# Two feed-forward layers whose weights are split in place, from scratch copies that the attention's last steps make

## The chip, the cores and the metric

The kernel runs as one program on one core of one Trainium2 chip. The metric is the device time of one execution in microseconds (us), taken as the median of several runs. The trace comes from one profiled execution. Engines are named as in the profile: PE (TensorE) multiplies, PEld is its weight load, DVE is VectorE, ACT is ScalarE, POOL is GpSimd, and SP is the queue that issues most DMAs.

## The reference

Two transformer layers over x, 4096 tokens of 256 features, all in float32. Each sublayer takes a layer norm of x and adds its output to x.

```python
x = x + _L0_attn_ref(_layernorm(x), Wq, bq, Wk, bk, Wv, bv, Wo, bo)   # 16 heads of 16, full softmax over 4096
x = x + _L0_ffn_ref(_layernorm(x), gate_w, w1, b1, w2, b2, sw1, sb1, sw2, sb2)
x = x + _L1_attn_ref(_layernorm(x), ...)                              # linear attention with a gate
x = x + _L1_ffn_ref(_layernorm(x), router_w, router_b, w1, b1, w2, b2, sw1, sb1, sw2, sb2)
```

The first feed-forward has a shared expert `relu(x @ sw1 + sb1) @ sw2 + sb2` with 1024 hidden columns, and two experts of the same size, of which each token takes the one that its gate scores higher. The second has a shared part of 2 x 512 hidden columns with silu, and 64 experts of 64 hidden columns, of which each token takes eight with their softmax weights. Together the weights of the two feed-forward layers are 6 MB and 10 MB.

## The kernel before

The program is a row of phases, each with its own semaphores: `setup_phase`, `qkv0_phase`, `attention_phase`, `ffn0_phase`, `qkv1_phase`, `kv1_phase`, `out1_phase` and `moe_phase`. A phase ends with a barrier over all engines, POOL clears the phase's semaphores, and there is a second barrier (`PhaseSemaphores.__exit__`, lines 93 and 94). A phase that calls `sem.start()` then gives all its semaphores a first value of one: POOL adds it to one after the other (line 86), and a barrier follows (line 87), before which no engine does anything of the phase. Six phases do so, with 32, 24, 37, 21, 39 and 50 semaphores (qkv0, attention, ffn0, qkv1, out1 and moe).

Every product of the feed-forward layers is made of three matmuls with operands cut in a high and a low part (`product3`, lines 56 to 58): ACT copies the float32 value to a high part in fp32r, and DVE subtracts that from the value and writes the low part. Weights need the same cut once. `WeightCut` does that through a small ring of staging places: SP loads item n to place n mod ring (line 938) when DVE has done with item n - ring, ACT writes the high part (942), DVE the low part (946). Each item is 128 partitions x 1024 values, 512 KB, with a few smaller ones. `weights.ready` makes an engine wait for the low part of the last item.

**Attention.** 64 steps, eight pairs of heads by eight blocks of 512 keys. PE makes the scores for the maximum (line 724) and for the exponential (737, 745) and the product with the values (757), DVE takes the maxima (837), ACT the exponentials (814). Per step SP issues, in this order: the loads of the keys of the block three steps ahead (`load_k`, lines 659 and 664), in two steps of sixteen also the next pair's queries (`load_q`), and then `load_shift` (682 and 688), which brings the negated maxima of the next step into the rows of its keys when POOL has cut them; PE waits for that before the next step's exponential scores. POOL stores NUM and DEN at each step's end. SP's stream of the last sixteen steps is written out separately from the loop before it.

**ffn0_phase.** Eight blocks of 512 tokens. Before the first block, the "front" of block 0 runs: reciprocal of den, quotient, its cut (`o_hi`, `o_lo`), the output projection, the sum x1, the layer norm (mean, centre, square, variance, std, reciprocals, scale, hi, lo) and the gate. SP loads num, den, x, then nine bias and gate columns, and then the twelve weight items over three staging places. ACT and DVE wait for all nine columns first, do the weights' cuts with parts of the front between them, and PE begins block 0 after `weights.ready`. In a block, 24 chunks of 128 hidden columns go through `hidden` (6 matmuls), ACT twice, DVE, and `output` (6 matmuls) two chunks later; for the 16 routed chunks DVE first makes `chosen`. Between the chunks of a block stands the front of the next one, at fixed chunks. The blocks run in a loop of two per turn, and the last two are written out (`overlapped`).

**moe_phase.** Eight blocks again, of 40 chunks (8 shared, 32 pairs of experts), and a router. SP loads seven biases, and 23 weight items over four staging places, one of which is the buffer of x; when all cuts are done (`weights.ready(sp)`) it loads x of block 0 (line 1751). Then come the layer norm of block 0, the router's products (`head`) and the chunks. Per chunk ACT makes the silu (1883), DVE multiplies it by the token's weight for routed chunks (1981), ACT cuts the high part (1889), DVE the low part (1984), and PE makes `output` of the chunk two before.

qkv1_phase and out1_phase load four and three biases at their start, and wait for them only when they come to use them.

## Time and profile before

| | us |
|---|---|
| median of three runs | 4902.59 (4899.29 to 4906.36) |
| the profiled execution | 4904.38 |
| its span, first to last instruction | 4902.7 |
| PE busy | 4503.7 (92% of the span) |
| DVE busy | 3647.4 (74%) |
| ACT busy | 3162.0 (64%) |
| POOL busy | 538.8 (11%) |
| first DMA of ffn0, of qkv1, of moe | 2803.48, 3463.42, 3797.22 |

PE is busy 92% of the span, and the stretches where it isn't lie at the ends and starts of the phases. The mean granted TensorE clock is 0.955 of full speed. The DMAs move 165 MB in all, a mean of 34 GB/s. A busy share is a mean over phases with different limits, so the places where PE stands still are to be read one by one.

### The profile page before, as it was taken

The page shows a single profiled execution, that of the slowest core. Times are in us where ns is not written, and L with a number is a line of the kernel's source. Part 1 is how long each engine was busy: PE and PEld are TensorE (multiplying, and loading weights), DVE is VectorE, ACT ScalarE, POOL GpSimd, SP SyncE. Part 2 cuts the span into 40 slices and gives each one's busy share as a digit, 9 for nine tenths or more (in the row PEclk, how much of TensorE's full clock was granted, in tenths as well). Part 3 has the DMA queues.
Part 4 walks back from the last instruction along what each step waited for, and adds up shares of the span by engine and source line. Part 5 has one row for each costly group of instructions (what it writes and reads, how often), then busy time and mean ns, then how long its engine had stood idle before and what let it go on. Part 6 is the DMA issues. An engine that isn't in the chain of part 4 may idle for free. (4 is left out here: it accounts for less than half of the span.)

```text
span 4902.7 us, 107872 instructions
## 1 busy us (share of the span) xinstructions
PE 4503.7 (92%) x36227; PEld 2730.8 (56%) x36227; DVE 3647.4 (74%) x3699; ACT 3162.0 (64%) x5605; POOL 538.8 (11%) x1382
## 2 busy tenths in 40 slices
PE   6589999999999999999999789999874499999999
PEld 4344444444444444444444367777553378778777
DVE  4599999999998999999999765655446444444454
ACT  2158888888887888888888644444553344444444
POOL 3501111111111111111111100000000000000000
PEclk8789999999999999999999889999987699999999
DMA  4611110201202002120020120000101400000000
GB/s 162 197 29 21 26 25 18 34 18 22 34 17 34 18 18 34 21 33 21 18 33 18 39 69 26 28 23 14 36 13 60 96 13 13 13 13 13 13 5 14
DMA packets 216402, 165.36 MB, mean 34 GB/s; under 512 B 127728, under 2 KB 167328, under 8 KB 215104
## 3 DMA queue, kind: packets, MB, share of 16 engines
q1 hardware_dynamic: 199584, 151.15, 13.1%
q0 software_dynamic: 16384, 8.42, 0.7%
q8 instruction: 273, 4.47, 0.4%
q14 instruction: 161, 1.32, 0.1%
HBM read 103.63 MB, written 55.05 MB: 32 GB/s over the span
## 5 line engine op out<-in xcount | busy, mean ns | idle before, releaser
L837 DVE TENSOR_REDUCE PM<-A 128x2 f32<-128x1024 f32 x2092 | 2456.7, 1220 | 91.0 <-PE A L724 58.2
L814 ACT ACTIVATE PR<-SB 128x512 f32<-128x512 f32 x4100 | 2120.8, 603 | 360.6 <-PE SB L737 347.2
L757 PE MATMUL PV<-PR,VH 128*32 128x256 f32 x16384 | 1292.5, 386 | 2.4 <-issue 2.4
L724 PE MATMUL A<-QST,KA 48*128 48x512 f32 x4184 | 1193.2, 475 | 66.8 <-DMA QF<-QFD 41.7
L757 PEld LDWEIGHTS PV<-PR,VH 128*32 128x32 f32 x16384 | 432.9, 110 | 555.3 <-issue 367.8
L724 PEld LDWEIGHTS A<-QST,KA 48*128 48x128 f32 x4184 | 426.7, 187 | 524.0 <-issue 454.6
L737 PE MATMUL SB<-KST,QST 50*128 50x512 f32 x3075 | 687.6, 411 | 0.2
L737 PEld LDWEIGHTS SB<-KST,QST 50*128 50x128 f32 x3075 | 386.6, 186 | 207.8 <-ACT PR L814 204.8
L1984 DVE TENSOR_TENSOR m_h_lo<-m_h_full,m_h_hi 128x512 fp32r<-128x512 f32 x320 | 221.5, 692 | 285.1 <-ACT m_h_hi L1889 284.8
L745 PE MATMUL SB<-KF,QF 99*32 99x512 bf16 x4100 | 415.7, 384 | 5.5 <-issue 4.3
L1889 ACT CAST m_h_hi<-m_h_full 128x512 fp32r<-128x512 f32 x320 | 198.5, 620 | 245.5 <-DVE m_h_full L1981 243.4
L1981 DVE TENSOR_TENSOR m_h_full<-m_h_full,m_c 128x512 f32<-128x512 f32 x256 | 175.2, 684 | 235.4 <-ACT m_h_full L1883 205.0
L1883 ACT ACTIVATE m_h_full<-m_h,m_b 128x512 f32<-128x512 f32 x256 | 175.6, 686 | 195.3 <-PE m_h L58 194.6
L1195 DVE SCALAR_TENSOR_TENSOR chosen<-gate_out,h_ps 128x512 f32<-128x512 f32 x128 | 87.1, 680 | 181.3 <-PE h_ps L58 181.3
L896 POOL DMA_DIRECT2D NUM<-OS x256 | 126.6, 494 | 864.2 <-ACT OS L825 721.0
L1134 ACT ACTIVATE h_full<-chosen,b 128x512 f32<-128x512 f32 x128 | 92.4, 722 | 198.1 <-DVE chosen L1195 197.4
L56 PE MATMUL m_h<-ln_hi,moe_w_hi 128*128 128x512 f32 x512 | 208.7, 408 | 0.0
L57 PE MATMUL m_h<-ln_lo,moe_w_hi 128*128 128x512 f32 x512 | 202.8, 396 | 0.0
L56 PE MATMUL m_y<-m_h_hi,moe_w_hi 128*128 128x512 f32 x512 | 201.9, 394 | 0.0
L58 PE MATMUL m_h<-ln_hi,moe_w_lo 128*128 128x512 f32 x512 | 201.8, 394 | 0.0
L58 PE MATMUL m_y<-m_h_hi,moe_w_lo 128*128 128x512 f32 x512 | 201.5, 394 | 0.0
L57 PE MATMUL m_y<-m_h_lo,moe_w_hi 128*128 128x512 f32 x512 | 200.3, 391 | 0.0
(297 smaller groups left out, 5548.2 us busy)
## 6 DMA issues: line engine op xcount, KB each, us to landing
QST<-QS SPq DMA_DIRECT2D x54, 256.0 KB, 8.9
KA<-KAD SPq DMA_DIRECT2D x402, 32.0 KB, 1.8
KST<-KS SPq DMA_DIRECT2D x402, 32.0 KB, 1.9
QS<-parts SPq DMA_DIRECT2D x16, 512.0 KB, 5.7
KS<-parts SPq DMA_DIRECT2D x16, 512.0 KB, 4.7
KAD<-dealt SPq DMA_DIRECT2D x16, 512.0 KB, 3.5
m_x<-X3T SPq DMA_DIRECT2D x16, 512.0 KB, 3.7
KF<-KFD SPq DMA_DIRECT2D x402, 16.0 KB, 1.8
```

Of the source, the lines that this page charges most:

```text
L56: nc.tensor.matmul(out, w[0], x[0], start=first, stop=False)
L57: nc.tensor.matmul(out, w[0], x[1], start=False, stop=False)
L58: return nc.tensor.matmul(out, w[1], x[0], start=False, stop=last)
L724: return nc.tensor.matmul(A[:, u % 2 * 2 + e, :], keys, QST[rows, slot, j * TB:(j + 1) * TB], start=True, stop=True)
L737: nc.tensor.matmul(SB[:, s_bank(v), :], QST[rows, slot, c * P:(c + 1) * P], KST[rows, nb % K_SLOTS, :], start=True, stop=True).then_inc(s_ ...
L745: mm = nc.tensor.matmul(SB[r * 2 * HD:(r + 1) * 2 * HD, s_bank(v), :], QF[0:FINE_ROWS, slot, at:at + 2 * HD], KF[0:FINE_ROWS, nb % K_SLOTS ...
L757: mm = nc.tensor.matmul(PV[at:at + 2 * HD, 0:HB], VH[:, slot, e, c, :], PR[:, (2 * c + e) % P_SLOTS, b * HB:(b + 1) * HB], start=(c == 0), ...
L814: nc.scalar.activation(PR[:, v % P_SLOTS, :], SB[:, s_bank(v), :], ACT.Exp, scale=SCALE).then_inc(s_free, 1)
L837: nc.vector.tensor_reduce(PM[:, par, :, i, j:j + 1], A[:, u % 2 * 2:u % 2 * 2 + 2, :], AX.X, ALU.max).then_inc(a_free, 1)
L1883: nc.scalar.activation(h_full[:, c % RING, :], h_ps[:, c % 2, :], ACT.Silu, bias=bias).then_inc(full_ready, 1)
L1889: nc.scalar.copy(h[0][:, c % RING, :], h_full[:, c % RING, :]).then_inc(hi_ready, 1)
L1984: nc.vector.tensor_tensor(h[1][:, c % RING, :], h_full[:, c % RING, :], h[0][:, c % RING, :].bitcast(F32), ALU.subtract).then_inc(lo_ready, 1)
```

## The change

- `PhaseSemaphores.start` deals the first values out to five engines in turn.
- `weight_copies`: nineteen DMAs copy all feed-forward weights from the inputs to scratch tensors in device memory (F1, F2, RW, S1, S2, W1, W2). Eighteen of them make 16 MB, most of 1 MB each, and RW has 64 KB. W1 is stored as 256 rows of 4096 values, so its copy writes runs of 64 values (256 bytes).
- `constant_loads`: 21 DMAs load all later biases and gate columns to a lasting buffer `constants`. The loads of them in ffn0, qkv1, out1 and moe are gone, with their waits; only the two loads of `L1_ffn_b2` stay in moe.
- SP issues these 40 DMAs in the last sixteen steps of the attention, two or three after each step's `load_shift`, and waits for all of them at the end of its stream.
- `WeightCut` has no staging: an item is loaded from the scratch copy to the place of its low part, ACT writes the high part, and DVE subtracts in place. Each item has a semaphore of its own, and SP issues all loads without waiting.
- ffn0: items 0 to 3 (the shared expert) are cut between the parts of block 0's front, items 4 to 11 within block 0 at the chunks in `CUTS`, and PE waits per item (`ready(pe, n)`). The columns' differences and sums are made after `o_lo`. The first two blocks are written out.
- moe: x is loaded first. Items 0 to 3 are cut within block 0's layer norm, items 4 to 22 within block 0 (`CUTS`). The shared experts' weights now come ahead of the routed ones in the list. Tail 0 and head 1 are written out.
- Numbers of semaphores per phase as above: 32, 25, 45, 20, 38 and 69, of which each engine gives a fifth its first value.

```diff
+def overlapped_from_first(eng, body):
+    for slot in range(2):
+        body(0, slot, slot, 2)
+    with eng.Fori(1, NB // 2 - 1) as half:
...
     def start(self):
+        nc = self.nc
+        engines = (nc.gpsimd, nc.sync, nc.scalar, nc.vector, nc.tensor)
         for n, s in enumerate(self.held):
             if n not in self.from_zero:
-                self.nc.gpsimd.sem_inc(s, FIRST)
-        self.nc.all_engine_barrier()
+                engines[n % len(engines)].sem_inc(s, FIRST)
+        nc.all_engine_barrier()
...
+def weight_copies(d):
+    copies = [(d["F1"][0], d["L0_ffn_sw1"]), (d["F2"][0], d["L0_ffn_sw2"]), (d["RW"], d["L1_ffn_router_w"])]
+    for e in range(2):
+        copies += [(d["F1"][e + 1], d["L0_ffn_w1"][e]), (d["F2"][e + 1], d["L0_ffn_w2"][e])]
+        copies += [(d["S1"][e], d["L1_ffn_sw1"][e]), (d["S2"][e], d["L1_ffn_sw2"][e])]
+    per_expert = d["W1"].rearrange("n (e h) -> e n h", h=D // 4)
+    for g in range(0, 64, 16):
+        copies.append((per_expert[g:g + 16], d["L1_ffn_w1"][g:g + 16]))
+    for g in range(4):
+        rows = slice(g * 1024, (g + 1) * 1024)
+        copies.append((d["W2"][rows], d["L1_ffn_w2"].rearrange("e h n -> (e h) n")[rows]))
+    return copies
+
+def constant_loads(d, K):
+    loads = [(K["bo"], column(d["L0_attn_bo"])), (K["f0_b1"][:, 0:8], column(d["L0_ffn_sb1"])),
...
@@ attention_phase, SP, the last 16 of 64 steps @@
                         step(pair * NB + nb, pair, hp, nb, (pair + 1) % HPAIRS)
+                        for dst, src in early[hp * NB + nb::2 * NB]:
+                            sp.dma_start(dst, src, allow_slow_non_contiguous=True).then_inc(ahead_moved, 16)
+                sp.wait_ge(ahead_moved, count(16 * len(early)))
...
@@ class WeightCut @@
-    def load(self, sp):
-        ring = len(self.places)
-        for n, (src, _, _) in enumerate(self.items):
-            if n >= ring:
-                sp.wait_ge(self.lo_done, count(n - ring + 1))
-            sp.dma_start(self.staged(n), src).then_inc(self.loaded[n % ring], 16)
+    def load(self, sp, n):
+        src, _, low = self.items[n]
+        sp.dma_start(low.bitcast(F32), src).then_inc(self.loaded[n], 16)
 
     def hi(self, act, n):
-        act.wait_ge(self.loaded[n % len(self.places)], count(n // len(self.places) * 16 + 16))
-        self.nc.scalar.copy(self.items[n][1], self.staged(n)).then_inc(self.hi_done, 1)
+        act.wait_ge(self.loaded[n], count(16))
+        _, high, low = self.items[n]
+        self.nc.scalar.copy(high, low.bitcast(F32)).then_inc(self.hi_done, 1)
 
     def lo(self, dve, n):
         dve.wait_ge(self.hi_done, count(n + 1))
-        self.nc.vector.tensor_tensor(self.items[n][2], self.staged(n), self.items[n][1].bitcast(F32),
+        _, high, low = self.items[n]
+        self.nc.vector.tensor_tensor(low, low.bitcast(F32), high.bitcast(F32),
                                      ALU.subtract).then_inc(self.lo_done, 1)
 
-    def ready(self, eng):
-        eng.wait_ge(self.lo_done, count(len(self.items)))
+    def ready(self, eng, n):
+        eng.wait_ge(self.lo_done, count(n + 1))
...
@@ ffn0_blocks @@
+        CUTS = {2: 4, 3: 5, 4: 6, 6: 7, 9: 8, 10: 9, 11: 10, 14: 11}
...
                 load_sums(0)
                 load_x(0, 0)
-                col(bo[:, :], d["L0_attn_bo"])
...
-                weights.load(sp)
-                weights.ready(sp)
+                for n in range(PER):
+                    weights.load(sp, n)
+                for n in range(PER, len(items)):
+                    weights.load(sp, n)
                 sp.wait_ge(o_lo, count(1))
...
                 def hidden(i, slot, c):
+                    if first(i) and c % HC == 0:
+                        weights.ready(pe, c // HC * PER + 1)
...
                 def output(i, c):
                     e, k = divmod(c, HC)
+                    if first(i) and k % (HC // 2) == 0:
+                        weights.ready(pe, e * PER + 2 + k // (HC // 2))
...
+                for part in ("projection", "mean", "variance"):
+                    front(0, 0, part)
                 pe.wait_ge(diffed, count(4))
-                for part in ("projection", "mean", "variance", "gate"):
-                    front(0, 0, part)
-                weights.ready(pe)
-                overlapped(pe, blocks)
+                front(0, 0, "gate")
+                overlapped_from_first(pe, blocks)
...
-                for n in range(len(items)):
-                    weights.hi(act, n)
-                    front(0, 0, {1: "o_hi", 4: "square", 6: "std", 9: "hi"}.get(n))
-                overlapped(act, blocks)
+                for n, part in enumerate(("o_hi", "square", "std", "hi")):
+                    front(0, 0, part)
+                    weights.hi(act, n)
...
                 def blocks(half, i, slot, following):
                     for c in range(C):
+                        if first(i) and c in CUTS:
+                            weights.lo(dve, CUTS[c])
...
-                dve.wait_ge(consts, count(CONST_LOADS))
+                for part in ("den0", "den1", "den2", "den3", "quotient", "o_lo"):
+                    front(0, 0, 0, part)
...
@@ moe_phase and moe_blocks @@
+                cols = slice(g * G * EH, (g + 1) * G * EH)
+                items.append((d["W1"][k * P:(k + 1) * P, cols], *[v[:, k, cols] for v in w1]))
...
+        CUTS = {0: (4,), 1: (5,), 2: (6,), 3: (7,), 4: (8,), 5: (9,), 7: (10,), 10: (11,), 11: (12,), 12: (13,), 15: (14,),
+                18: (15,), 19: (16,), 20: (17,), 23: (18,), 26: (19,), 27: (20,), 28: (21,), 31: (22,)}
...
             head(0, False)
-            with eng.Fori(0, NB - 1) as i:
+            tail(0, True)
+            head(1, True)
+            with eng.Fori(1, NB - 1) as i:
...
-                weights.load(sp)
-                weights.ready(sp)
                 sp.dma_start(x[:, :, :], x3_dram[:, :, 0:TB]).then_inc(x_loaded, 16)
+                for n in range(2):
+                    weights.load(sp, n)
+                for p in range(2):
+                    sp.dma_start(b2_raw[p * 64:(p + 1) * 64, :], d["L1_ffn_b2"]).then_inc(bias_loaded, 16)
+                for n in range(2, EARLY):
+                    weights.load(sp, n)
+                for n in range(EARLY, len(items)):
+                    weights.load(sp, n)
...
-                for n in range(len(items)):
-                    weights.lo(dve, n)
-                weights.ready(dve)
                 ln.vector_centre(dve, 0)
+                weights.lo(dve, 0)
                 for part in range(2):
                     ln.vector_reciprocal(dve, 0, part)
                 ln.vector_scale(dve, 0)
+                weights.lo(dve, 1)
+                weights.lo(dve, 2)
                 ln.vector_lo(dve, 0)
+                weights.lo(dve, 3)
```

## Rows read from the trace of the kernel before

**Rows 1.** Windows: start and end us, length, busy us of each engine, clock, DMA share, GB/s.

```profile
2600.00:2700.00 100.00, 99.93 (x1124) 47.30 (x1126) 98.15 (x87) 86.35 (x169) 11.58 (x37) 1.00 0.08 15
2854.20:2932.20 78.00, 75.70 (x318) 59.78 (x319) 44.16 (x56) 34.73 (x52) 0.00 (x0) 0.99 0.11 34
3800.00:3850.00 50.00, 0.00 (x0) 0.00 (x0) 25.42 (x25) 21.87 (x24) 0.00 (x0) 0.50 0.99 214
3871.30:3999.30 128.00, 127.46 (x539) 102.52 (x540) 58.85 (x96) 58.49 (x87) 10.34 (x32) 0.97 0.02 5
```

**Rows 2.** Timeline of SP's queue, two attention steps: start us, us of issuing, DMA, how many.

```profile
2731.05 2.41 SPq L682 DMA_DIRECT2D KST<-NM  x4
2733.50 1.90 SPq L688 DMA_DIRECT2D KF<-NF  x3
...
2769.42 2.41 SPq L682 DMA_DIRECT2D KST<-NM  x4
```

**Rows 3.** Instructions of line 86 on POOL, whole span.

```profile
L86 POOLq EVENT_SEMAPHORE  x203: 17/17/17, 21.3 to 3796.9; - x102
```

**Rows 4.** Waits of SP: us in total, times, longest.

```profile
SPq L87 <- PEq L87: 17.2, 6, 4.1
```

**Rows 5.** Ends of the attention's streams, line 652: duration ns, start us.

```profile
L652 SPq DRAIN  x1: 369/369/369, 2773.8 to 2773.8; - x1
...
L652 POOLq DRAIN  x1: 10515/10515/10515, 2788.7 to 2788.7; - x1
```

**Rows 6.** Timeline, start of the first feed-forward: start us, us, instruction, idle before.

```profile
2803.93 0.46 SPq L1023 DMA_DIRECT2D den<-DEN  x1
...
2811.91 0.47 SPq L1019 DMA_DIRECT2D gate_cols<-in_L_ffn_gate_w  x1
...
2815.24 6.58 DVE L1155 RECIPROCAL den<-den 128x256 f32<-128x256 f32 x4
...
2823.12 1.04 ACT L1115 CAST ln_hi<-num 128x1024 fp32r<-128x1024 f32 x1 [4.53 <-DVE num L1158]
...
2825.27 1.22 DVE L1163 TENSOR_TENSOR ln_lo<-num,ln_hi 128x1024 fp32r<-128x1024 f32 x1
...
2841.25 0.69 ACT L172 ACTIVATE ln_sq<-front_ps,eps 128x512 f32<-128x512 f32 x1 [0.23 <-PE front_ps L137]
...
2849.78 1.23 DVE L163 TENSOR_TENSOR ln_lo<-ln_xc,ln_hi 128x1024 fp32r<-128x1024 f32 x1
...
2854.21 0.79 PE L56 MATMUL h_ps<-ln_hi,f_w_hi 128*128 128x512 f32 x1 [0.23 <-DVE f_w_lo L946]
```

**Rows 7.** Timeline, start of the mixture of experts.

```profile
3797.22 0.36 SPq L1743 DMA_DIRECT2D r_bias<-in_L_ffn_router_b  x1
...
3814.47 1.04 ACT L942 CAST moe_w_hi<-m_h_full 128x1024 fp32r<-128x1024 f32 x1 [0.53 <-DMA m_h_full<-in_L_ffn_w]
...
3815.55 1.23 DVE L946 TENSOR_TENSOR moe_w_lo<-m_h_full,moe_w_hi 128x1024 fp32r<-128x1024 f32 x1 [0.35 <-ACT moe_w_hi L942]
...
3849.52 0.37 SPq L1751 DMA_DIRECT2D m_x<-X3T  x1
3853.41 3.75 PE L130 MATMUL m_turn<-m_x,ones 128*128 128x512 f32 x4 [65.67 <-DMA m_x<-X3T]
...
3869.93 1.23 DVE L163 TENSOR_TENSOR ln_lo<-ln_xc,ln_hi 128x1024 fp32r<-128x1024 f32 x1 [1.11 <-ACT ln_hi L177]
3871.31 0.39 PE L56 MATMUL m_turn<-moe_rw_hi,ln_hi 128*128 128x64 f32 x1 [7.86 <-DVE ln_lo L163]
```

**Rows 8.** DMA issues: how many, KB each, median us to landing.

```profile
den<-DEN SPq DMA_DIRECT2D x8, 512.0 KB, 4.8
...
ln_sq<-in_L_ffn_w SPq DMA_DIRECT2D x4, 512.0 KB, 5.5
```

**Rows 9.** Groups by line: busy us, mean ns, idle before, releaser.

```profile
L1883 ACT ACTIVATE m_h_full<-m_h,m_b 128x512 f32<-128x512 f32 x256 | 175.6, 686 | 195.3 <-PE m_h L58 194.6
L1981 DVE TENSOR_TENSOR m_h_full<-m_h_full,m_c 128x512 f32<-128x512 f32 x256 | 175.2, 684 | 235.4 <-ACT m_h_full L1883 205.0 <-PE m_c L1802 30.4
```

More of the change, by code:

```diff
@@ L46, in feature_major @@
     return ap.rearrange("(k p) n -> p k n", p=P)
+def overlapped_from_first(eng, body):
+    for slot in range(2):
+        body(0, slot, slot, 2)
+    with eng.Fori(1, NB // 2 - 1) as half:
+        for slot in range(2):
+            body(half, half * 2 + slot, slot, 2)
+    for slot in range(2):
+        body(NB // 2 - 1, NB - 2 + slot, slot, 1 - slot)
 def column(ap):
@@ L1592, in _ @@
                 copy_o(0)
-                act.wait_ge(consts, count(48))
                 with act.Fori(0, NB // 2 - 1) as i:
@@ L1807, in output @@
                     w, k = (s2, c) if c < SC else (w2, c - SC)
+                    if first(i):
+                        weights.ready(pe, 1 + c // (SC // 2) * 3 + 2 if c < SC else 7 + k // 8 * 4 + 2 + k % 8 // 4)
                     pe.wait_ge(lo_ready, count(i * C + (c + 1)))
@@ L1834, in head @@
                 def head(i, finish):
+                    if first(i):
+                        weights.ready(pe, 0)
                     pe.wait_ge(ln.lo_ready, count(i + 1))
@@ L1879, in chunk @@
                 def chunk(i, c):
+                    if first(i):
+                        for n in CUTS.get(c, ()):
+                            weights.hi(act, n)
                     act.wait_ge(h_done, count(i * C + (c + 1)))
@@ L1977, in chunk @@
                 def chunk(i, c):
+                    if first(i):
+                        for n in CUTS.get(c, ()):
+                            weights.lo(dve, n)
                     if c >= SC:
@@ L2018, in _ @@
                                         ALU.subtract).then_inc(b_cut, 1)
-                for n in range(len(items)):
-                    weights.lo(dve, n)
-                weights.ready(dve)
                 ln.vector_centre(dve, 0)
+                weights.lo(dve, 0)
                 for part in range(2):
@@ L2044, in program @@
              "ones": sb("ones", [P, P], F32), "eps": sb("eps", [P, 1], F32)}
+        constants = sb("constants", [P, sum(CONSTANTS.values())], F32)
+        at = 0
+        for name, n in CONSTANTS.items():
+            K[name] = constants[:, at:at + n]
+            at += n
         with ExitStack() as weights:
```

161 lines of the change are left out of this document (81 added, 80 removed).

## The prediction

> **What bounds the kernel now.** I read the windows first, to see which stretches an engine fills. In the attention PE is busy 99.9 us of 100 and DVE 98 [rows 1]: nothing of this change touches either, so that phase can only be disturbed. In block 0 of each feed-forward phase PE is busy 75.7 of 78 us and 127.5 of 128 [rows 1]: PE bounds them. The 50 us in front of the second one are the opposite: PE does nothing, its clock is granted at 0.50, DVE and ACT are half busy, and the DMA engines are busy 99% of the time at 214 GB/s [rows 1]. That is the weight load with its small ring. So the gain must come from the time between a phase's barrier and PE's first block, and the timelines of the two starts [rows 6, 7] are where it is read. Between phases there is also the start barrier: SP waits there 17.2 us in six phases [rows 4], while POOL gives 203 semaphores their first value [rows 3].
>
> **Semaphores.** 17.2 us for 203 increments is 0.085 us each; some of that is the barrier, which stays, so I take 0.080. After the change the engines work side by side and the longest share counts: 7, 5, 9, 4, 8 and 14 increments, 47 in all. 156 fewer at 0.080 is 12.5 us: 2.2 in ffn0 (28 fewer), 2.9 in moe (36), 7.4 in the other four (92). All engines stand at this barrier, so all of it is on the path. The rate of the four other engines isn't shown. Below, it can be as fast as POOL or faster (1 to 2 us more at most); above, I allow twice POOL's time, 0.16 us each, and then 47 x 0.08 = 3.8 us are lost again. I take POOL's rate.
>
> **ffn0, up to block 0.** Now the first reciprocal of den starts at 2815.24, after the last gate column, which SP issued at 2811.91, though den was issued at 2803.93 [rows 6]. Afterwards nothing but den holds it. With the barrier 2.2 us earlier den is issued at 2801.7, lands 4.8 us later [rows 8], and the reciprocals start at 2806.5. From their start to PE's first product of block 0 are now 2854.21 - 2815.24 = 39.0 us [rows 6]. Of these go: 1.1 us between the end of `o_hi` (2824.16) and `o_lo` (2825.27), filled by two cuts of weights; about 1.8 us of the 9.1 between the end of std (2841.94) and that of the layer norm's low part (2851.01), since the two cuts between the reciprocals and one more are gone and one (1.2 us on DVE, beside 1.05 on ACT, so 0.2 net) stays; and 0.2 us of the last wait for the cut weights. That leaves 35.9, and block 0 starts at 2842.4, 11.8 us earlier. Items 0 to 3 are cut where DVE waits for PE or ACT anyway. The bound on the other side: twelve loads of weights are queued right behind den and x, and if they share the engines with den it lands like a weight load, 5.5 us, or up to 2 us later.
>
> **ffn0, in block 0.** Eight cuts, 1.23 us of DVE and 1.04 of ACT each (the size of those in [rows 7]), go into a block in which DVE is free for 33.8 of 78 us and ACT for 43.3 [rows 1]. On average they are hidden. But three stand at chunks 2, 3 and 4, where DVE has a reciprocal of 1.65 us too (6.58 for four [rows 6]) and a low part of 0.68: 3.6 us for a chunk, against 78 / 24 = 3.25 for the mean chunk with all its extra work, and less for these, which have none on PE. Chunk 10 has a cut, the two operations of x1, and two more of 0.7 each. `output` runs two chunks late, and that forgives one such delay but not three. Between 0 (the two chunks of slack take all) and 8 us (every cut waits about 1 us) I take 3.4. ffn0 gains 8.4.
>
> **moe, up to block 0.** SP's first DMA goes from 3797.22 to 3794.3, and it is x. Alone, x took from 3849.52 to PE's start at 3853.41, 3.9 us, and from there to the router's first product at 3871.31 it was 17.9 us [rows 7]. DVE has items 1 and 2 (half size, 0.68 us each) between scale and low part while ACT makes the high part: 0.3 us. The two `L1_ffn_b2` loads come behind x and two small items and are cut while PE makes the mean (3.75 us), so they cost nothing; if they land later than that they cost what they are late, up to 2 us. The router starts at 3794.3 + 3.9 + 17.9 + 0.3 = 3816.4 and no longer at 3871.3: 54.9 us earlier. What covers the load of 10 MB now is block 0 itself: at the 214 GB/s of before it takes 50 us, and its last item is cut at chunk 31 of 40, some 100 us into the block. The next block's x stands behind all weights in SP's queue, lands near 3850, and is asked for at chunk 12, about 3816 + 12 x 3.2 = 3855, with the router's products ahead of it some us more: 5 us to spare, no more. PE's clock is low when it starts on either kernel (0.50 before, and 0.97 is the mean of that block 0 [rows 1]), so it takes no part in the difference.
>
> **moe, in block 0.** Nineteen cuts into 128 us with 69 us of DVE and 69.5 of ACT free [rows 1]. Here ACT and DVE wait for each other in each routed chunk: cut 1.04, silu 0.69, DVE's product 0.68, high part near 0.65 make 3.1 us with its handovers near 3.6 [rows 7, 9], against 3.2 us a chunk (128 / 40). Runs of three cuts (chunks 10 to 12, 18 to 20, 26 to 28) get late by some 1.5 us, which the two chunks of lag forgive, except at 18 to 22, where the next layer norm's two reciprocals and scale are on DVE too: about 5 us late against 3 forgiven. With something for chunk 4, where ACT loads tables, I take 4, between 0 and 10 (half a us for each cut). moe gains 50.9.
>
> **The attention.** A step takes 38.4 us (2731.05 to 2769.42), SP's last shift of one is issued at 2735.4 and the next one not before 2769.4 [rows 2]; in between stand only key loads, which are wanted more than a step later. So the copies have 34 us a step, less some 3 for the key loads' bytes. The first steps copy two times 1 MB. The trace has no copy from device memory to device memory. The nearest rows are the weight loads, with 256-byte runs in moe, 214 GB/s together [rows 1]: 10 us for 2 MB. Even at a third of that the next shift goes undisturbed. POOL's stores may share the engines with key loads behind a copy, but POOL has nothing due for some 20 us. The last copy is issued when SP's stream ends now, 2773.8, and POOL drains from 2788.7 for 10.5 us [rows 5]; so SP's new wait is hidden by 25 us. I take nothing, with 3 us as the upper end (0.2 us a step).
>
> The Trainium skill ("DMA: Bandwidth & Descriptors", "Why a DMA increments its semaphore by 16 and not by 1") has a rule that could speak against this: a DMA is spread over the largest number up to 16 that divides the slowest dimension of both its sides, and a copy without such a dimension runs on one engine. By that rule these copies, with 256, 512 or 1024 rows or 16 experts ahead, get all sixteen, and the sum stays; were one flattened, the third rival below would be the result. No row here shows which, as all transfers of the trace have one side in SBUF.
>
> **Sum.** 7.4 + 8.4 + 50.9 = 66.7 us. The sum is made against the profiled execution, 4904.38, which is 1.8 above the median of the three runs; both move alike. 4902.6 - 66.7 = 4835.9. qkv1 and out1 gain nothing from their missing loads, since they wait for them behind their first work; the extra waits of PE and the larger clears (69 semaphores, not 50) are tenths. What this kernel's measurement can tell from no change is 0.2%, some 10 us.
>
> **Rivals.** First, the cuts in block 0 cost more than I give them. For it: the chunk of 3.6 us against 3.2, and runs of three. Against it: both engines are half idle in the block [rows 1]. If each of the 27 cuts holds PE for its 1.04 us of ACT, it is 28 us and not 7.4, so 4856; half of that, 4845. It shows as idle PE with DVE's low part as releaser. I give 4845 to 4858 a chance of 0.16.
>
> Second, queueing: num, den, x and b2 share the engines with the weight loads behind them, or the second block's x is late. Den and x would be 2 us late each, the second x by the 50 us load being, say, 65: 7 us. That gives 4840 to 4847, part of the range anyway. 0.10.
>
> Third, slower than before: a copy runs on too few DMA engines and the next `load_shift` stands behind it. 214 GB/s over sixteen engines is 13.4 GB/s each [rows 1]. On one engine 1 MB takes 78 us, all copies 1250 us, where sixteen steps last 614: the attention ends some 640 us later and the time is near 5475. It decides where two copies don't fit in 31 us, which is below 68 GB/s or five engines. Against it: key and weight loads are spread. 0.05.
>
> Fourth, the change doesn't do what it says, because PE's start in moe hangs on something else that I don't see, or the dearer side of the increments comes with the first rival: gain under 10 us 0.02, otherwise 4858 to 4880 0.04.
>
> **Chances and range.** My forecast, 4827 to 4845, has 0.63 (its lower end is with no stalls in both blocks: 4828). Slower by over 0.2% 0.05, within 0.2% 0.02, faster 0.93. With 0.63 + 0.10 + most of the first rival the range 4825 to 4855 holds 0.8 and more; its lower end takes in the stalls at zero and increments faster than POOL's, its upper end stalls of 8 and 10, increments at twice the price, and 2 us of queueing: 66.7 - 10.6 - 3.8 - 2 = 50.3, 4852.
>
> **What the profile would show.** SP's waits at the start barrier near 5 us in all. The first reciprocal of den near 2803 (2806.5 less the 3.5 us gained in the two phases ahead), and 35.9 us from it to the first product of block 0. In moe x as the first DMA, 22 us to the router, and block 0 at 128 us plus some 4 of idle PE. Attention steps of 38.4 us to the end. I am wrong if shifts land late (PE idle in the last sixteen steps), if PE's idle time in either block 0 is over 10 us, or if the router starts more than 24 us after SP's first DMA.

## The result, and the profile after

The changed kernel takes 4852.29 us, the median of four runs (4846.32 to 4852.49), against 4904.48 for the kernel before on the same chip: a ratio of 0.9894, with a 95% interval of 0.9882 to 0.9906. That is 52 us less; the prediction had 4836, or 67 us less. The profiled execution is the fastest of the four, 4846.32 us with a span of 4844.7, so it gained 58.0 us on the one profiled before.

To see where the 58 us come from, I cut both traces at the same events: the first and the last copy of an attention step's sums (ACT, `OS<-PV`), the first product of h in each feed-forward, the last store of X2T and moe's first DMA. The third column is the prediction's, with its semaphore term dealt out by the increments that each phase saves.

| stretch | before, us | after, us | gain forecast | gain measured |
|---|---|---|---|---|
| start to first copy of sums | 327.63 | 323.29 | 3.5 | 4.3 |
| first to last copy of sums | 2454.95 | 2460.03 | 0 | -5.1 |
| to ffn0's first product | 71.63 | 60.42 | 11.8 | 11.2 |
| to the last X2T store | 603.54 | 614.07 | -3.4 | -10.5 |
| to moe's first DMA | 339.47 | 332.02 | 6.8 | 7.5 |
| to moe's first product of h | 79.20 | 26.97 | 52.0 | 52.2 |
| to the end | 1026.28 | 1027.90 | -4.0 | -1.6 |

The waits of SP at the start barrier [rows 4], us in total, times, longest; then the start of ffn0 that answers to [rows 6] and that of moe that answers to [rows 7]:

```profile
SPq L100 <- PEq L100: 5.2, 6, 1.4
```

```profile
2802.53 0.39 SPq L1073 DMA_DIRECT2D num<-NUM  x1
2802.97 0.47 SPq L1074 DMA_DIRECT2D den<-DEN  x1
...
2807.65 6.59 DVE L1207 RECIPROCAL den<-den 128x256 f32<-128x256 f32 x4 [24.13 <-DMA den<-DEN]
...
2843.74 0.63 PE L67 MATMUL h_ps<-ln_hi,f_w_hi 128*128 128x512 f32 x1
...
3789.83 0.39 SPq L1789 DMA_DIRECT2D m_x<-X3T  x1
...
3793.78 3.78 PE L143 MATMUL m_turn<-m_x,ones 128*128 128x512 f32 x4 [11.59 <-DMA m_x<-X3T]
...
3811.68 0.39 PE L67 MATMUL m_turn<-moe_rw_hi,ln_hi 128*128 128x64 f32 x1 [7.86 <-DVE ln_lo L176]
```

The barrier wait fell from 17.2 to 5.2 us. The reciprocals of den wait for den alone, and from the first of them to block 0 it is 2843.74 - 2807.65 = 36.1 us. In moe the router starts 21.9 us after SP's first DMA. So both starts went as forecast, and the question is what happened in the two stretches with the large minus: the attention and ffn0's blocks.

PE's waits in moe's block 0 after the change, us in total, times, longest:

```profile
PE m_y L67 <- DVE m_h_lo L2045: 1.8, 3, 1.0
PE m_c L1852 <- DVE cw L2032: 1.0, 1, 1.0
```

These and two shorter ones make 3.4 us. The stretch from the router's first product of block 0 to that of block 1, before and after (columns as in [rows 1]):

```profile
3871.30:4002.40 131.10, 130.56 (x553) 105.01 (x554) 60.77 (x98) 59.56 (x88) 10.34 (x32) 0.97 0.02 5
3811.70:3946.50 134.80, 131.41 (x553) 104.30 (x554) 81.89 (x118) 76.12 (x108) 12.56 (x32) 0.97 0.11 37
```

It is 3.7 us longer, with PE idle for 3.4 us where it was 0.5. The six blocks between that and the last take 127.7 us each and not 128.0, and the last is 0.3 shorter too, so the last row of the table hides most of what block 0 lost: 3.7 lost, 2.1 gained. What made the later blocks shorter isn't isolated. The load of moe's weights moves 379 GB/s from 3799.8 to 3819.8, and the 10 MB are through some 34 us after moe's first DMA, where the prediction took 50 for them from the 214 GB/s of before. The DMAs of moe's start make 7985 packets now; they made 28642, of which 22880 were under 512 bytes. Which part of the speed comes from the copies' longer rows and which from the missing ring, no run separates.

The issues of the copies, size each and median us to landing, and SP's queue in one of the steps that carry them:

```profile
W<-in_L_ffn_w SPq DMA_DIRECT2D x4, 1024.0 KB, 6.1
S<-in_L_ffn_sw SPq DMA_DIRECT2D x4, 512.0 KB, 3.9
```

```profile
2736.09 0.60 SPq L772 DMA_DIRECT2D W<-in_L_ffn_w  x1
2737.05 3.32 SPq L772 DMA_DIRECT2D constants<-in_L_ffn_b  x1
...
2770.10 2.42 SPq L736 DMA_DIRECT2D KST<-NM  x4
```

A copy of 1 MB lands in 6.1 us, 172 GB/s for one DMA, so by estimate it runs on many engines: the 214 GB/s of [rows 1] are 13.4 for each of sixteen. The next shift is due 34 us later. The fifteen steps from the sixteenth-last copy of sums to the last take 578.2 us, as before (578.1). What the prediction cited from the Trainium skill ("DMA: Bandwidth & Descriptors", on the spreading over the slowest dimension) agrees with this landing, which doesn't tell many engines from all sixteen.

ffn0's blocks are read from SP's stores of X2T, start us and us of issuing:

```profile
3003.45 0.40 SPq L1089 DMA_DIRECT2D X2T<-f_x  x1
3081.07 0.40 SPq L1089 DMA_DIRECT2D X2T<-f_x  x1
3158.40 0.40 SPq L1089 DMA_DIRECT2D X2T<-f_x  x1
```

The distances are 77.62 and 77.33 us. In the trace of before the same stores stand 76.61 and 76.33 apart, and so on in turn for all: seven blocks cost 7.2 us more, although neither the code of those blocks nor the granted clock (1.00) differs. In the attention the loss isn't at the copies at all. It lies ahead of them, mostly in steps 15, 31 and 47, the ones at which the engines' loop of sixteen steps jumps back or ends. The turn at step 15 in windows (engines' busy us, PE's clock, DMA share, GB/s), and PE's two waits in it, at 906 and at 927 us:

```profile
905.00:910.00 5.00, 4.07 (x27) 2.03 (x27) 2.45 (x2) 2.10 (x4) 2.91 (x6) 0.50 0.33 76
...
925.00:930.00 5.00, 2.77 (x22) 1.84 (x22) 1.16 (x2) 0.85 (x2) 0.00 (x0) 0.83 0.27 49
930.00:935.00 5.00, 5.00 (x34) 2.12 (x35) 3.11 (x4) 2.88 (x6) 0.00 (x0) 0.50 0.00 0
935.00:940.00 5.00, 5.00 (x47) 2.26 (x39) 3.20 (x3) 2.88 (x7) 0.00 (x0) 0.64 0.00 0
940.00:945.00 5.00, 5.00 (x60) 2.54 (x58) 4.68 (x6) 4.26 (x9) 1.29 (x7) 1.00 0.06 5
```

```profile
PE A L781 <- issue: 3.4, 1, 3.4
PE PV L814 <- issue: 2.8, 1, 2.8
```

PE stands still twice with nothing to wait for but its own next instruction: for 3.4 us at the jump, and for 2.8 us some 20 us behind it, in the middle of a step. Each time the clock is then granted at 0.50, the lower of its two levels (1.2 GHz), over the next window. With both, this step takes 51.9 us and not 38.5. The kernel before has the same turns, at 43.1, 48.7 and 47.6 us; its stands at the jumps are 2.8, 2.8 and 3.1 us, and the second stand is missing in its first turn, the shortest.

### The profile page after: what moved, and what is told of

It is laid out like the page before. It is cut to its first block and busy times, and to the rows that moved or that the text cites. A ratio compares the mean times of both kernels' runs of the same rounds, so it can differ in the third digit from the quotient of the medians.

```text
span 4844.7 us, 107645 instructions
## 1 busy us (share of the span) xinstructions
PE 4509.8 (93%) x36227; PEld 2729.0 (56%) x36227; DVE 3645.8 (75%) x3699; ACT 3157.8 (65%) x5605; POOL 541.7 (11%) x1382
## 5 line engine op out<-in xcount | busy, mean ns | idle before, releaser
L814 PE MATMUL PV<-PR,VH 128*32 128x256 f32 x16384 | 1293.4, 387 | 3.5 <-issue 3.5
L814 PEld LDWEIGHTS PV<-PR,VH 128*32 128x32 f32 x16384 | 433.2, 110 | 557.9 <-issue 367.0
L794 PE MATMUL SB<-KST,QST 50*128 50x512 f32 x3075 | 689.8, 411 | 5.1 <-ACT PR L871 4.6
L794 PEld LDWEIGHTS SB<-KST,QST 50*128 50x128 f32 x3075 | 387.9, 187 | 213.3 <-ACT PR L871 209.3
L802 PE MATMUL SB<-KF,QF 99*32 99x512 bf16 x4100 | 414.9, 384 | 1.2 <-ACT PR L871 1.2
L1939 ACT ACTIVATE m_h_full<-m_h,constants 128x512 f32<-128x512 f32 x320 | 219.6, 686 | 255.4 <-PE m_h L69 254.2
L1186 ACT ACTIVATE h_full<-chosen,constants 128x512 f32<-128x512 f32 x128 | 92.3, 721 | 198.4 <-DVE chosen L1247 198.4
```

The costliest lines, as they stand in the source:

```text
L794: nc.tensor.matmul(SB[:, s_bank(v), :], QST[rows, slot, c * P:(c + 1) * P], KST[rows, nb % K_SLOTS, :], start=True, stop=True).then_inc(s_ ...
L802: mm = nc.tensor.matmul(SB[r * 2 * HD:(r + 1) * 2 * HD, s_bank(v), :], QF[0:FINE_ROWS, slot, at:at + 2 * HD], KF[0:FINE_ROWS, nb % K_SLOTS ...
L814: mm = nc.tensor.matmul(PV[at:at + 2 * HD, 0:HB], VH[:, slot, e, c, :], PR[:, (2 * c + e) % P_SLOTS, b * HB:(b + 1) * HB], start=(c == 0), ...
L1939: nc.scalar.activation(h_full[:, c % RING, :], h_ps[:, c % 2, :], ACT.Silu, bias=bias).then_inc(full_ready, 1)
```

## The experiments

Theory A is about ffn0: the buffers' places in SBUF set TensorE's pace. The new buffer `constants` moves every later one up by 1664 bytes, and as `bo`, `b1`, `b2` and `gate_cols` are gone from ffn0, the gate's and layer norm's buffers behind them move by 1472 only. Theory S came up with the first runs: the first values that TensorE now deals out stand in its instruction stream ahead of the attention's loop and make it longer.

**Old places.** After, with padding:

```diff
         with ExitStack() as weights:
+            weights.enter_context(nc.sbuf_tensor("pad", [P, 608], F32))
...
+        sb("pad_ffn0", [P, 48], F32)
         b2_sum = sb("b2_sum", [P, KC], F32)
```

> The changed kernel with 608 more columns of padding behind the constants (in all phases ahead of moe) and 48 in ffn0, so that in these phases each buffer lies exactly 4096 bytes above its place in the kernel before, instead of 1472 or 1664. Theory A, the addresses set the pace of TensorE: the steady blocks of ffn0, 77.3 to 77.6 us in the changed kernel, come back to the 76.3 to 76.6 us of before, and the kernel is some 8 us faster than the changed one (about 4843); if the 6 to 7 us that the attention lost are of the same kind, about 4837. Theory B, the pace has nothing to do with addresses (the operands' placement, the code, or a difference from one run to the next): the blocks stay at 77.3 to 77.6 or differ by chance, and the time stays at 4846 to 4853.

4842.95 us (4828.20 to 4848.41), ratio 0.9864, 0.9836 to 0.9893. The stores of X2T:

```profile
3010.65 0.40 SPq L1090 DMA_DIRECT2D X2T<-f_x  x1
3087.22 0.40 SPq L1090 DMA_DIRECT2D X2T<-f_x  x1
3163.55 0.40 SPq L1090 DMA_DIRECT2D X2T<-f_x  x1
```

They stand 76.57 and 76.33 apart: the padding mends ffn0, as theory A has it. The attention wasn't cured, it took 2470.2 us.

**First values alone.** Before, with the changed `start` and nothing else:

```diff
+        engines = (nc.gpsimd, nc.sync, nc.scalar, nc.vector, nc.tensor)
         for n, s in enumerate(self.held):
             if n not in self.from_zero:
-                self.nc.gpsimd.sem_inc(s, FIRST)
+                engines[n % len(engines)].sem_inc(s, FIRST)
```

> The kernel before with only the first values of semaphores dealt out to five engines. By the prediction's term: 12.5 us faster, so 4892 beside the 4904 of before. Rival, the waits at the start barriers are hidden or come back as waits for the first DMA: under 5 us. For the attention, whose start this moves 1 to 2 us ahead: theory B has its length between the copies of the sums of the first and last step within the spread from run to run; if it always comes out longer than 2455.0 us when it starts earlier, the start matters. The steady ffn0 blocks stay at 76.3 to 76.6 by theory A, since no address changes.

4898.47 us (ten runs), ratio 0.9993, 0.9980 to 1.0007: some 4 us and not 12.5, and not told from no change. In its trace the stretches outside the attention are 16.8 us shorter than before, and the attention is 6.9 us longer (2461.9). So a saving of the forecast size is there, and the attention gives much of it back. If the stretches outside are as long in the other nine runs, the attention takes 12.8 us more at the median, an estimate.

**The buffer alone, and the copies alone.** Before, with 413 unused columns; then the same with the copies and the loads of constants in the attention, used by nothing:

```diff
+        sb("constants", [P, 413], F32)
         with ExitStack() as weights:
```

> The kernel before with an unused buffer of 413 columns behind eps, which moves every later buffer up by 1664 bytes, and nothing else. Theory A: the steady ffn0 blocks take 77.3 to 77.6 us in place of 76.3 to 76.6, and the kernel is 7 to 14 us slower than before (4911 to 4918). Theory B: within 0.1 percent of before (4900 to 4909).

```diff
+        ahead_moved = sem("ahead_moved")
+        early = weight_copies(d) + constant_loads(d, K)
...
+                        for dst, src in early[hp * NB + nb::2 * NB]:
+                            sp.dma_start(dst, src, allow_slow_non_contiguous=True).then_inc(ahead_moved, 16)
+                sp.wait_ge(ahead_moved, count(16 * len(early)))
```

> The kernel before with the constants' buffer, the 19 copies and the 21 loads in the attention's last sixteen steps as in the changed kernel, but used by nothing: ffn0, qkv1, out1 and moe are as before. The prediction's term for the copies in the attention is 0 to 3 us, so it stands within 3 us of the run with the unused buffer alone, and its last sixteen steps keep 38.4 to 38.7 us each. Rival, the copies disturb the attention by 6 us or more: it is that much slower than the run with the unused buffer.

4904.29 us (ratio 0.9998, 0.9986 to 1.0011) and 4900.96 (0.9995, 0.9984 to 1.0007). The buffer moves everything by the same 1664 bytes and ffn0 keeps its 76.3 to 76.6: it isn't a buffer's place that counts but the distance between some of them, which only the changed kernel alters. As I had written it, theory A was wrong on this run. The copies are free: the attention with them took 2451.1 us, without them 2456.1.

**Two paddings.** After, with 64 bytes in ffn0 and 32 in moe:

```diff
+        sb("pad_ffn0", [P, 16], F32)
         b2_sum = sb("b2_sum", [P, KC], F32)
...
+        sb("pad_moe", [P, 8], F32)
         b2_sum = sb("m_b2_sum", [P, KC], F32)
```

> The changed kernel with two paddings: 64 bytes in ffn0, which put the layer norm's parts (ln_hi, ln_lo: the moving operands of h_ps) at 32 modulo 128 bytes where the changed kernel has 96, and 32 bytes in moe, which put them at 32 where the changed kernel has 0 (the kernel before has 32 and 64). In ffn0 no buffer gets its old address back, as it did in the run with the old addresses. Theory A1, what counts is the operands' place modulo 128 bytes, and 32 is a good one: ffn0's steady blocks take 76.3 to 76.6 us and moe's, 128.0 in both kernels, fall to about 126.3 (some 300 products per block at 0.2275 in place of 0.233 us), so the kernel is 7 + 14 us faster than the changed one, about 4832. Theory A2, it is the distance between particular buffers: ffn0 stays at 77.3 to 77.6 or lands in between, and moe stays at 128.0.

4842.63 us, ratio 0.9879 (0.9862 to 0.9896). ffn0's blocks stay at 77.4 to 77.65, so the place modulo 128 bytes is not it (A1 falls). But moe, from its first product of h to the end, took 1021.7 us in place of 1027.9, and its steady blocks 126.8 us in place of the changed kernel's 127.7 (not 128.0, as the expectation has it for both kernels): there the distance from the layer norm's parts to the weights had become 0 modulo 256 bytes, where it was 224.

**TensorE's attention written out.** The last kernel, with

```diff
-                in_steps(pe, step)
+                for t in range(STEPS):
+                    step(t // (2 * NB), t // NB % 2, t % NB)
```

> The kernel of the run with the two paddings, with TensorE's 64 attention steps written out, in place of a loop of four turns of sixteen steps; the other engines keep their loops. Theory, the steps at the loop's turns (43 to 52 us against 38.2 to 38.7, at steps 15, 31 and 47) are long because TensorE fetches its first instructions after a jump late (2.8 us of idle time put down to its own issue) and the granted clock then stands at 0.50 to 0.64 for 10 us: the three steps come down to under 39 and the kernel gains 22 to 38 us, the sum of their excess in the profiles so far. Rival, the other engines' jumps, at the same step, hold it up just the same, or the longer stream stalls elsewhere: the sum over the attention changes by less than 10 us.

4819.71 us, 23 less. The attention took 2447.8 us and the three turns are 40.9, 45.2 and 45.3 us. What is left belongs to ScalarE, which still loops (waits of ACT and of PE in the ten microseconds of the first turn):

```profile
ACT PR L872 <- issue: 2.5, 1, 2.5
```

```profile
PE SB L802 <- ACT PR L872: 1.8, 1, 1.8
```

Both sides of the expectation had a part: TensorE's own stream costs most, and ScalarE's jump comes forward when TensorE's is gone.

**TensorE deals none, and eleven more.** The kernel with the two paddings and four engines in `start`; then the same with eleven increments put back into TensorE's stream:

```diff
-        engines = (nc.gpsimd, nc.sync, nc.scalar, nc.vector, nc.tensor)
+        engines = (nc.gpsimd, nc.sync, nc.scalar, nc.vector)
```

```diff
+                for n in range(11):
+                    alone(pe, passed)
                 pe.wait_ge(rows_set, count(2))
```

> The kernel of the run with the two paddings, with the first values dealt out to four engines instead of five: TensorE gives none, so its instruction stream is as in the kernel before. Theory S, the attention's 7 us (from 2451 to 2456 us between the first and last copy of the sums in three profiles with POOL alone, to 2460 to 2470 in three with five engines) come from these instructions in TensorE's stream, which move the loop's code against what is fetched at a time: the attention is back at 2451 to 2456 and the kernel 5 to 8 us faster than that with the two paddings. Theory R, the attention's length varies by such amounts from run to run: same time within 3 us, with an attention anywhere from 2450 to 2470.

> The kernel of the run in which TensorE deals out no first values, with eleven increments of a semaphore that nobody waits for put into TensorE's stream at the start of the attention: as many instructions as its share of the first values of qkv0 (6) and of the attention (5) was. Theory S, what lengthened the attention is the place of the loop in TensorE's instruction stream: the attention goes from 2450 us back to 2460 to 2470 and the kernel from 4830 to 4840 to 4845, though the increments take well under 1 us themselves. Rival S2, it is TensorE's part in the starts (when it arrives at the barriers) and not its stream: the attention stays at 2450 to 2456.

4829.55 us (4824.73 to 4840.03), ratio 0.9863 (0.9846 to 0.9881), and 4840.43 (4839.19 to 4851.73), ratio 0.9877 (0.9860 to 0.9893). The intervals overlap, so the traces have to carry it. The copies of the attention's sums on ACT: duration ns, first and last start, first for the kernel in which TensorE deals none, then with the eleven put back:

```profile
L882 ACT COPY OS<-PV x64: 406/408/410, 323.3 to 2773.6; 128x256 f32<-128x256 f32 x64
```

```profile
L884 ACT COPY OS<-PV x64: 406/407/408, 326.9 to 2795.8; 128x256 f32<-128x256 f32 x64
```

2450.3 and 2468.9 us. All attentions in which TensorE loops, by what stands ahead of the loop in its stream:

| in TensorE's stream | first to last copy of sums, us | excess of the three turns over 38.5 |
|---|---|---|
| no first values (before, buffer alone, unused copies, moe alone, deals none, other distances) | 2455.0, 2456.1, 2451.1, 2450.2, 2450.3, 2453.0 | 19 to 26 |
| eleven more instructions (after, first values alone with ten, old places, two paddings, eleven more) | 2460.0, 2461.9, 2470.2, 2469.0, 2468.9 | 27 to 38 |

The groups don't overlap; the means are 2452.6 and 2466.0. But each length is that of one execution, and the executions of one kernel differ as much: the trace with TensorE dealing none is the fastest of its four, that with the eleven put back the slowest, 11.3 us above its median, and 8.5 of the 27.0 us between the two lie outside the attention. So this pair gives no size. What it does show is where PE stands still. PE's waits in the attention, us in total, times, longest, without the eleven and then with them:

```profile
PE A L781 <- issue: 9.5, 3, 3.3
PE SB L802 <- issue: 1.4, 1, 1.4
PE PV L814 <- issue: 0.8, 1, 0.8
```

```profile
PE A L781 <- issue: 9.2, 3, 3.3
PE PV L814 <- issue: 6.1, 2, 3.0
PE SB L794 <- ACT PR L873: 3.8, 3, 1.4
PE SB L794 <- issue: 2.5, 1, 2.5
```

The three stands at the jumps (`A`) are alike. The others move to another instruction: 22 to 26 us behind a jump from the fine scores (L802) to the product with the values (L814), and in the middle of the sixteen steps from that product to the scores (L794). All eleven traces show it: those without have their stands at the first pair of places (one has none in the middle), those with at the second. The profile puts some of those at L794 down to ScalarE, whose exponentials free the bank for them. All stands of over half a us other than the jumps' three, whoever ended them, come to 1.4 to 6.2 us without and 8.1 to 13.3 with, while the jumps' come to 8.7 to 9.5 and 9.2 to 9.7. Increments that nobody waits for bring this pattern back, so it is their place in TensorE's stream and not the dealing; the 13 us between the means are a rough size.

**moe's part alone.** The kernel with the unused copies, with the changed moe (`StagedCut` is the old `WeightCut`, which ffn0 keeps):

```diff
-        weights = WeightCut(nc, sem, items, places)     # moe
+        weights = WeightCut(nc, sem, items)             # moe, in place
...
-        weights = WeightCut(nc, sem, items, places)     # ffn0
+        weights = StagedCut(nc, sem, items, places)     # ffn0
```

> The kernel with the unused copies, with the changed moe phase in the place of the old one: ffn0, qkv1, out1 and the first values by POOL alone are as before. The prediction's terms for moe without the semaphores: 52.0 us earlier start, 4 given back in block 0, so 48 us less from moe's first DMA to the end than the 1105.5 us of before. By the profile of the changed kernel, which spent 1054.9 us there, it should be 1054.9 plus some 2.3 for the first values by POOL. Rival, ffn0's own change made room for moe's (copies, constants): more than 1060.

4848.80 us in one run. From moe's first DMA to the end its trace has 1054.8 us, as the changed kernel (1054.9) and 50.7 less than before: moe's gain needs nothing of ffn0's. The 2.3 us that the expectation adds for the first values lie ahead of moe's first DMA and so outside this stretch.

**Both written out, and other distances.** To the kernel in which TensorE deals none: TensorE's and ScalarE's attention written out and 48 columns of padding in ffn0; or, with all loops kept, 112 columns in ffn0 and 72 in moe.

```diff
-                in_steps(pe, step)
+                for t in range(STEPS):
+                    step(t // (2 * NB), t // NB % 2, t % NB)
...
-                in_steps(act, step)
+                for t in range(STEPS):
+                    step(t // (2 * NB), t // NB % 2, t % NB)
...
-        sb("pad_ffn0", [P, 16], F32)
+        sb("pad_ffn0", [P, 48], F32)
```

```diff
-        sb("pad_ffn0", [P, 16], F32)
+        sb("pad_ffn0", [P, 112], F32)
...
-        sb("pad_moe", [P, 8], F32)
+        sb("pad_moe", [P, 72], F32)
```

> The kernel of the run in which TensorE deals out no first values, with the attention of TensorE and of ScalarE written out (64 steps), and in ffn0 a padding of 192 bytes, which gives ln_hi and ln_lo the same distance from the weights and from h as in the kernel before (256 modulo 512 bytes). By what the run with TensorE alone written out showed (at each turn ScalarE then had 2.5 us of idle time of its own issue, and TensorE waited 1.8 us for it), steps 15, 31 and 47 come down to under 39.5 us, the attention to 2433 or less, 17 us shorter than with both loops; and ffn0's steady blocks to 76.3 to 76.6, 7 us in all. Sum: about 4806. Rival, VectorE's turn takes their place (its issue showed 0.3 us): a part of the 17 us stays. Rival for ffn0, the distance is not what counts: 77.3 to 77.6.

> The kernel of the run in which TensorE deals out no first values, with 448 bytes of padding in ffn0 and 288 in moe: ln_hi and ln_lo lie at a distance of 0 modulo 512 bytes from the weights in ffn0 (256 in the kernel before, 64 in the changed one) and of 256 in moe (480 in the changed one, 0 in the three last kernels, where moe from the first product of m_h to the end took 1021.7 us in place of 1027.9). Theory D, what counts is this distance modulo 256 bytes, with 0 a good one: ffn0's blocks take 76.3 to 76.6 and moe keeps 1021.7. Rival D2, modulo 512 or more: one or both come out slow (77.4; 1026 to 1028).

4827.45 us (0.9853, 0.9837 to 0.9869): no gain on the kernel it was made from. The turns are gone (39.1, 39.1 and 39.7 us), but now the steps take 38.8 to 39.1 us in turn in place of 38.4 to 38.7, and the attention 2457.1. On the mean of the other steps that is 38.99 against 38.58 us, some 25 us over the attention (the 39.07 us and 37 us of the next expectation take every second step for all). The forecast of 4806 was 21 us off. PE's waits in this attention come to 2.0 us, so why the steps are longer stays open. ffn0 came to 76.4 and 76.6.

The other distances took 4822.94 us in one run, ffn0's blocks at 76.3 to 76.6 and moe 1021.7. With all kernels, the distance from the layer norm's parts to the weights, modulo 256 bytes:

| distance mod 256 | ffn0's steady blocks, us | moe, first product of h to the end, us | moe's steady blocks, us |
|---|---|---|---|
| 0 | 76.3 to 76.6 (9 kernels) | 1021.7 to 1022.5 (7 kernels) | 126.8 |
| 64 | 77.3 to 77.6 (after) | | |
| 128 | 77.3 to 77.65 (4 kernels) | | |
| 160 | | 1026.1 to 1026.6 (4 kernels) | 128.0 |
| 224 | | 1027.9 to 1028.0 (3 kernels) | 127.7 |

The four kernels at 160 have the old moe, without cuts in block 0; that row differs from the other two in more than the distance.

**The parts together.** The kernel with the other distances, and TensorE's attention written out:

```diff
-                in_steps(pe, step)
+                for t in range(STEPS):
+                    step(t // (2 * NB), t // NB % 2, t % NB)
```

> The kernel of the run with the other distances (448 bytes of padding in ffn0, 288 in moe, no first values by TensorE), with TensorE's 64 attention steps written out and all other loops kept. That kernel took 4822.9 us with an attention of 2453.0. Theory, the parts add: the attention comes to 2448 us as in the first run with TensorE written out, the slow turns there being ScalarE's, ffn0's blocks keep 76.3 to 76.6 and moe 1021.8: about 4817. Rival, as with both engines written out, the longer stream makes each step longer (39.07 us in place of 38.5 were measured there, 37 us over the attention): the attention is 2455 us or more and the kernel no faster than 4823.

4813.76 us (4808.98 to 4815.56), ratio 0.9816 with 0.9803 to 0.9830: 88 us below the kernel before on that chip (4901.61) and some 38 below the changed one. The attention takes 2439.0 us in the trace, of the fastest of the five runs, better than I had expected:

```profile
L883 ACT COPY OS<-PV x64: 403/403/403, 321.0 to 2760.1; 128x256 f32<-128x256 f32 x64
```

What is left of the turns (43.5, 40.7 and 42.2 us) goes with ScalarE's jumps. PE's wait in the first:

```profile
PE SB L802 <- ACT PR L872: 1.6, 1, 1.6
```

## Why the prediction was right, and where it wasn't

The time fell within the range, but outside the forecast proper, 4827 to 4845, which had 0.63, and that it fell within is luck. 4852 is the sum that the prediction makes with all its allowances used up: stalls of 8 and 10 us, increments at twice the price, queueing. None of them came. It is also in the band of the first rival, whose cause, PE held up by every cut for 28 us in all, the traces don't show: both blocks together are 7.0 us longer. What used up the room were two losses that the prediction has no term for.

- **Semaphores.** 156 fewer increments at 0.080 us, 12.5 us. SP's barrier waits fell by 12.0. The trace of the kernel with this part alone shows 16.8 us gained outside the attention, but 6.9 lost within, and its median is only 4 us shorter, within the noise: "all of it is on the path" held for the barriers and not for the kernel.
- **ffn0 up to block 0.** 11.8 forecast, 11.2 measured; from the first reciprocal to block 0 36.1 us against 35.9.
- **ffn0, in block 0.** 3.4 forecast. From its first product to its store of X2T it takes 82.3 us against 79.0, 3.3 more; with the distance mended (four kernels) it is 80.6 to 81.9, against 78.4 to 79.0 in the five with the old ffn0. Part of that spread goes with the clock granted in the block's first ten microseconds (0.85 in the changed kernel, 0.94 before). At a high clock (0.96 to 0.99) the mended ones take 80.6 and the kernel with the first values alone 78.4, so the cuts cost some 2.2 us by this estimate, and the number 3.3 agrees with 3.4 by the help of the distance and the clock. PE's only new wait is one of 1.4 us for `h_lo`.
- **moe.** 54.9 to the router's first product with the barrier, 52.0 without; measured 52.2, and 50.7 with block 0 in the kernel with this part alone. Block 0 is 3.7 us longer, of which 2.9 are idle time of PE, where I gave the cuts 4: that term was right, though the table's last row has only 1.6, because the seven blocks behind it came out 0.3 us shorter each.
- **The copies.** Nothing forecast, nothing measured (the unused copies: 0.9995).

The first step that failed is the prediction's sentence on the attention, "nothing of this change touches either, so that phase can only be disturbed", with its "I take nothing": I asked only what the copies would do to the last sixteen steps. The first values put eleven instructions into TensorE's stream ahead of the loop, and that moved and lengthened the places inside the loop where TensorE stands still for its next instruction, not those at the jump. It cost 5 us in the profiled execution and 13 us between the means of the eleven traces.

The second is the term "ffn0 gains 8.4", which ended with block 0. The seven blocks behind it have unchanged code, and I priced them at nothing; by removing four small buffers the change altered a distance in SBUF, and they cost 7.2 us more.

Without these two, the profiled execution would have gained 58.0 + 5.1 + 7.2 = 70.3 us against the 66.7 forecast; of the 3.6 us over, 2.4 are in moe's blocks and most of the rest in the phases whose gain is the barriers' alone. The measured median has 52 and not 58; the profiled execution was the fastest of four. Outside the attention its trace gained 63.1 us, so if that holds for the others, their attention lost some 11 us, an estimate that no trace of theirs backs.

What stays open: which two buffers' distance it is and who collides with whom (the products of y, which read h and weights alone, whose distance is as before, are slower as well: from 3000 to 3150 us the first of each three takes 402 ns on the mean and not 395), why TensorE stands still longer at one place in its stream than at another, and why every step is longer with two engines written out.

## What to carry to other kernels

A change acts also on what it doesn't name: count the instructions that it puts ahead of a loop on the engine that is the bound, see whether the places where it waits for its own issue move, and count the bytes by which it moves buffers against each other. Look at the steady blocks before and after, whose code is the same: 1% there, over seven blocks, is as much as a shorter start. And where a loop of long steps runs at the bound, look at the turn: written out on the one engine whose jump showed, TensorE, it paid 9 to 23 us here, and on the next engine too it didn't.

## What the runs showed of the hardware

- The distance between buffers in SBUF, modulo 256 bytes, is worth 1.4% of ffn0's steady blocks (531.8 at 64 or 128 against 524.6 us at 0, for seven) and 0.7% of moe's (127.7 at 224 against 126.8 us at 0), at a clock of 1.00. Moving all buffers together by 1664 bytes changed nothing.
- A jump back costs TensorE 2.7 to 3.4 us of its own issue, ScalarE 2.5. In many turns TensorE stands a second time, for 0.7 to 3.4 us, 22 to 25 us behind the jump. In the turn shown, the granted clock was at half for some microseconds after each. A step of 38.5 us becomes one of 43 to 52.
- Ten or eleven instructions ahead of a loop change at which of its instructions TensorE stands, and for how long; the attentions of 2453 us were 13 us longer on the mean of five traces.
- In the changed moe the weight load moved 379 GB/s over twenty microseconds, where it was 214 GB/s with the ring and with 256-byte runs.
- A DMA from device memory to device memory of 1 MB landed in 6.1 us at the median of four, and sixteen steps with 16 MB of them are no longer than without.
